# Token rows over 128 partitions, one row index per transfer, and first tokens turned by TensorE

## The chip, the cores and the metric

The kernel runs on one core of one Trainium2 chip. The time is the device time of one execution in microseconds; lower is better.

## What is computed

The inputs are `x` and a context `ctx`, both (32, 512, 512) in float32: 16384 tokens of 512 features. Reference, cut to what matters:

```python
def _L0_xattn_ref(q, k, v):               # k = v = ctx
    def step(r, kv_t):                    # along the 512 tokens of a batch row
        r = 0.9 * r + kv_t                # kv_t = k * v
        return (r, r)
    ...
    return q * jnp.swapaxes(rs, 0, 1)

def _L0_ffn_ref(x, ...):
    h = jnp.einsum('bsd,dh->bsh', x, W_exp) + b_exp        # 512 -> 2048
    h = butterfly(h, up_weights, D_HIDDEN)                 # 11 stages
    h = jax.nn.gelu(h + up_bias, approximate=False)
    h = butterfly(h, down_weights, D_HIDDEN)
    return jnp.einsum('bsh,hd->bsd', h, W_con) + b_con + down_bias

x = x + _L0_xattn_ref(_layernorm(x), ctx, ctx)
x = x + _L0_ffn_ref(_layernorm(x), ...)
```

## The kernel before

**Fold.** Both butterflies are linear, so the kernel first folds them into the two weight matrices: into W_exp (512 x 2048) and W_con (2048 x 512). This is the start, some 148 us. TensorE does it in steps listed in `FOLD` (line 310): step n writes bank n mod 3 of three PSUM banks, and ACT (for a few steps VectorE) copies the bank out; TensorE waits for the copy of step n-3. The kinds stand in this order: WT (transposes of W_exp), low_up, high_up, turn_high, high_dn, turn_low, back, low_dn, sixteen (or four) steps each. Between low_up and high_up the matrix goes through DRAM: SP stores 16 pieces (`up_low_folded`, line 539) and loads them as `Z` in four quarters (line 545). Between these copies ACT and VectorE round weights to a high and a low part (`weights_hi`, `weights_lo`), and SP stores them as `w1_products` in DRAM (line 569); W_con's parts go to `w2_split` (line 580).

**Tokens.** A tile is 512 tokens: G = 4 groups by J = 4 row indices by Q = 32 tokens by 512 features. Group g lies on partitions 32g to 32g+31; group g of tile t starts at token g*4096 + t*128. There are 32 tiles, so a tile takes 128 successive tokens from each of four far stretches. `token_rows` (line 73) gives the view (g, t, i, j, d). One transfer `rows[g, t]` moves 32 partitions by 4 row indices by 512: 256 KB; a tile takes four. Two tiles (h = 0, 1) form a super-block; there are U = 16, in two buffers `x0` and `x1`. Context tile h = 0 is loaded to `kv`, h = 1 to `raw`; ACT squares it (`square`, line 869), VectorE turns it in 32x32 blocks, scans with 0.9 and turns it back (`scan_chunk`, line 1200), multiplies by the normalised x (`gate`) and normalises again (`normalise`, line 1260): it writes to `kvT`, and a 32x32 transpose puts that to `kv`. Then the blocks must change partition group: `move_xT` (line 510) issues 4 transfers of 64 KB, and 16 moves bring one tile to `raw`, turned. For the first super-block SP issues half of them (lines 582 to 593) and GpSimd the other half (`first_moves`, line 777). `tokens_hi`, `tokens_lo` and `token_sum` make from `raw` the seven operands `xop` of a Strassen-like product; the third token operand that ACT rounds needs the first `token_sum`.

**The main loop.** Each super-block has NP = 8 steps p. A step has NM = 7 products (m = 0 to 6, six matmuls of 128x512 each, line 1739) and 8 down parts of six matmuls (lines 1760 and 1773), in a fixed order: product, part, product, part and so on, two parts last; product m starts as piece 2m of the step's 15. A product reads one of RING = 8 weight buffers `w1r`, a down part `w2r`, one of two buffers for a step. SP's program is one list in order; a DMA waits on the issue of those ahead of it:

```python
def refill(u, p, m, last):
    n = p * NM + m + RING
    ...
    sp.wait_ge(m_done, u * PER + (p * NM + m + 1))
    load_w1(n % PER, n % RING)
```

In step 0 SP first loads the next context tile h = 0 to `kv`, and after product 6 (in the first super-block elsewhere) the next tile h = 1 to `raw`; in step 1 after m = 2 it stores the 8 output transfers of the super-block before, after m = 5 it loads the 8 x transfers of the next; then follows the load of `w2r`. VectorE's `stats1` of the new x stands in step 2. In steps 4 and 6 SP issues 16 moves each. In the last super-block only the output is stored. At the end the rows of tile 0 are stored by GpSimd (line 845), and those of tile 1 by SP and ACT as they come, two transfers of 64 KB each per row index (`store_last_row`, line 501).

**ACT's queue.** All its DMAs are: five for the first coefficients, of 16x2, 16x16, 8x16, 4x16 and 2x16 separate runs (lines 478 to 484), one of 4 runs (line 488), two bias vectors of 16 runs each, two biases broadcast to 128 partitions, `hc_up` with 128x32 runs (line 928), and 8 last stores of 32 runs. A run is one contiguous piece on both sides.

Of the kernel before, what the change touches and what calls it, by code (L numbers as in the profile page):

```python
# [24 lines left out]
def xattn_ffn_program(nc, x_in, ctx_in, w_exp, b_exp, up_w, up_bias, down_w, w_con, b_con, down_bias, out):  # L25
# [16 lines left out]
    G = 4  # L42
# [13 lines left out]
    FIRST_MOVES = MOVES // 2  # L56
# [26 lines left out]
    with es:  # L83
# [195 lines left out]
        first_moved = [sem("first_xTa_moved"), sem("first_xTb_moved")]  # L279
# [15 lines left out]
        def moved_by(u):  # L295
            return u * (MOVES * NX) + FIRST_MOVES * NX
# [96 lines left out]
        def kept(kind, i, bank):  # L393
# [12 lines left out]
            if kind == "turn_low":  # L406
                return LX[:, 1, 4 * i:4 * i + 4, :].rearrange("p a b -> p (a b)"), whole
            assert kind == "back"
# [107 lines left out]
        def _(sp):  # L516
            def load_tokens(dst, h, rows, t, loaded):
                for g in range(G):
                    sp.dma_start(dst[Q * g:Q * g + Q, J * h:J * h + J, :], rows[g, t]).then_inc(loaded, NX)
# [71 lines left out]
            sp.wait_ge(xn_turned, 2 * J)  # L591
            move_xT(sp, 1, 0, xT_moved[1])
            move_xT(sp, 1, 1, xT_moved[1])
# [14 lines left out]
            def store(u, par):  # L608
                for h in range(2):
# [4 lines left out]
                    for g in range(G):  # L614
                        sp.dma_start(out_rows[g, u * 2 + h], xs[par][Q * g:Q * g + Q, J * h:J * h + J, :])\
                          .then_inc(out_stored, NX)

            def load_x(u, par):
                wait(sp, out_stored, (u - 1) * (2 * G * NX))
# [3 lines left out]
            def body(u, par, first, last):  # L623
                go = not last
                for p in range(NP):
# [3 lines left out]
                    for m in range(NM):  # L629
# [7 lines left out]
                        if first and p == 0 and m == 4:  # L637
                            sp.wait_ge(first_moved[1], FIRST_MOVES * NX)
                            sp.wait_ge(xT_moved[1], moved_by(u))
# [19 lines left out]
                        if go and p == 4 and m < G:  # L659
                            if m == 0:  # L660
                                sp.wait_ge(xlo_ready, (u + 1) * NM)
                                sp.wait_ge(xn_turned, (u + 1) * (2 * J) + J)
                            move_xT(sp, 0, m, xT_moved[0])
                    if go and p == NP - 2:
                        sp.wait_ge(xn_turned, (u + 1) * (2 * J) + 2 * J)
# [8 lines left out]
            for j in range(J):  # L674
                store_last_row(sp, j, (0, 1))
# [1189 lines left out]
```

## Time and profile before

| | us |
|---|---|
| runs (3): median, lowest, highest | 2779.0, 2778.31, 2779.04 |
| the profiled execution, its own time | 2779.58 |
| its span, first to last instruction | 2777.8 |
| TensorE busy (matmuls) | 2739.9, 99% |
| VectorE busy | 2129.9, 77% |
| ACT busy | 1127.5, 41% |
| GpSimd busy | 401.5, 14% |
| SP queue's transfers, share of 16 DMA engines | 64.8% |

The busy shares are averages over a start of about 148 us in which the weights are folded, a main loop, and an end. The mean granted clock of TensorE is 0.993 of full speed.

### The profile page before, as it was taken

The numbers are of one execution on the slowest core, as the hardware profiler recorded it, in microseconds if no ns is written. First come the engines' busy times: TensorE is split into PE (matmuls) and PEld (weight loads), VectorE is DVE, ScalarE is ACT, GpSimd is POOL, SyncE is SP. The second block draws the span as 40 slices with busy tenths as digits, with TensorE's granted clock in tenths as the row PEclk, the third lists the DMA queues.
The fourth block names the chain that finished last, engine by engine and source line by source line (L and its number), as shares of the span: only waits on it lengthen the run. The fifth ranks groups of instructions, "written<-read, shape, count | busy, mean of one in ns | idle before, by whom it ended". The sixth has DMA issues, their size and how long they took to land.

```text
span 2777.8 us, 35037 instructions
## 1 busy us (share of the span) xinstructions
PE 2739.9 (99%) x12159; PEld 2259.3 (81%) x12159; DVE 2129.9 (77%) x3562; ACT 1127.5 (41%) x1707; POOL 401.5 (14%) x577
## 2 busy tenths in 40 slices
PE   8889999999999999999999999999999999999999
PEld 6668888888888888888888888888888888888887
DVE  8968787787878778787877878777787877788533
ACT  5653434334343443434343343433434343343432
POOL 4821011110101101010110201011020111101000
PEclk8999999999999999999999999999999999999999
DMA  9795675758567575856758475675847657585543
GB/s 272 261 294 176 195 201 174 217 154 252 158 199 205 167 225 154 236 171 191 212 164 233 153 223 183 179 221 160 241 151 222 186 173 225 159 243 152 183 151 99
DMA packets 294837, 542.57 MB, mean 195 GB/s; under 512 B 37430, under 2 KB 101078, under 8 KB 277766
## 3 DMA queue, kind: packets, MB, share of 16 engines
q1 hardware_dynamic: 287760, 536.82, 64.8%
q0 software_dynamic: 1488, 2.27, 0.4%
q10 hardware_dynamic: 5414, 1.25, 0.3%
q8 instruction: 99, 1.62, 0.3%
q14 instruction: 76, 0.62, 0.1%
HBM read 445.83 MB, written 60.82 MB: 182 GB/s over the span
## 4 chain that ended last, share of the span: by engine, by line
PE 94%; DVE 1%; POOL 0%; DMA 0%; ACT 0%; issue 0%; ACTq 0%; DVEq 0%; POOLq 0%
PE ps L1739 44%; PE ps L1760 25%; PE ps L1773 25%; DMA raw<-kv 0%; PE ps L1634 0%; PE ps L1840 0%; DVE w1r L1195 0%; DVE xop L1195 0%; DVE x L1252 0%; POOL raw L512 0%; DVE raw L1249 0%; DVE st L1255 0%; POOL x L760 0%; ACT xop L904 0%; PE ps L1639 0%
## 5 line engine op out<-in xcount | busy, mean ns | idle before, releaser
L1739 PE MATMUL ps<-xop,w1r 128*128 128x512 f32 x5376 | 1364.1, 389 | 2.5 <-DVE xop L1283 1.6
L1739 PEld LDWEIGHTS ps<-xop,w1r 128*128 128x128 f32 x5376 | 1008.9, 188 | 213.0 <-DVE xop L1283 2.3
L1760 PE MATMUL ps<-w2r,ghi 128*128 128x512 f32 x2048 | 630.5, 389 | 0.0
L1773 PE MATMUL ps<-w2r,ghi 128*128 128x512 f32 x2032 | 625.8, 389 | 0.0
L995 ACT ACTIVATE st<-ps 128x512 f32<-128x512 f32 x384 | 229.7, 598 | 839.8 <-PE ps L1739 839.8
L1389 DVE TENSOR_TENSOR x<-ps,x 128x512 f32<-128x512 f32 x508 | 348.9, 687 | 280.9 <-PE ps L1773 278.5
L1760 PEld LDWEIGHTS ps<-w2r,ghi 128*128 128x128 f32 x2048 | 384.4, 188 | 79.8
L1773 PEld LDWEIGHTS ps<-w2r,ghi 128*128 128x128 f32 x2032 | 381.2, 188 | 79.8 <-DVE glo L1412 0.4
L1407 DVE TENSOR_TENSOR g<-ps,st 128x512 f32<-128x512 f32 x384 | 262.8, 684 | 212.1 <-PE ps L1739 212.1
L999 ACT ACTIVATE g<-g,gelu_bias 128x512 f32<-128x512 f32 x384 | 275.4, 717 | 362.6 <-DVE g L1407 361.7
L1412 DVE TENSOR_TENSOR glo<-g,ghi 128x512 fp32r<-128x512 f32 x510 | 347.6, 702 | 79.2 <-ACT ghi L1013 79.2
L1760 PE MATMUL ps<-w2r,glo 128*128 128x512 f32 x1024 | 398.3, 389 | 0.0
L1773 PE MATMUL ps<-w2r,glo 128*128 128x512 f32 x1016 | 395.2, 389 | 0.0
L1013 ACT ACTIVATE ghi<-g 128x512 fp32r<-128x512 f32 x512 | 310.0, 629 | 12.2
L1006 ACT ACTIVATE g<-ps,gelu_bias 128x512 f32<-128x512 f32 x128 | 88.3, 690 | 355.5 <-PE ps L1739 355.5
L1760 PEld LDWEIGHTS ps<-w2r,glo 128*128 128x128 f32 x1024 | 192.2, 188 | 39.9
L1773 PEld LDWEIGHTS ps<-w2r,glo 128*128 128x128 f32 x1016 | 190.7, 188 | 39.6
L760 POOL TENSOR_TENSOR x<-x,bias_row 128x512 f32<-128x512 f32 x128 | 167.9, 1313 | 251.5 <-DVE kvT L1274 230.1
L743 POOL TENSOR_TENSOR ve<-mv,eps 128x4 f32<-128x4 f32 x32 | 11.4, 356 | 1250.1 <-DVE mv L1230 1250.1
L1216 DVE TENSOR_TENSOR_SCAN kvT<-decay,kvT 128x512 f32<-128x512 f32 x128 | 157.2, 1228 | 4.4
L1283 DVE TENSOR_TENSOR xop<-raw,xop 128x1024 fp32r<-128x1024 f32 x112 | 136.2, 1227 | 2.6 <-ACT xop L904 2.6
L904 ACT ACTIVATE xop<-raw 128x1024 fp32r<-128x1024 f32 x112 | 116.1, 1051 | 7.2 <-DVE raw L1299 7.2
(171 smaller groups left out, 1620.0 us busy)
## 6 DMA issues: line engine op xcount, KB each, us to landing
w1r<-w_products SPq DMA_DIRECT2D x889, 256.0 KB, 3.3
w2r<-w_split SPq DMA_DIRECT2D x126, 1024.0 KB, 4.9
x<-in_x_dram SPq DMA_DIRECT2D x128, 256.0 KB, 7.3
raw<-kv SPq DMA_DIRECT2D x496, 64.0 KB, 2.1
out_dram<-x SPq DMA_DIRECT2D x120, 256.0 KB, 4.1
kv<-in_ctx_dram SPq DMA_DIRECT2D x64, 256.0 KB, 7.4
raw<-in_ctx_dram SPq DMA_DIRECT2D x64, 256.0 KB, 5.4
wexp<-in_L_ffn_W_exp_dram SPq DMA_DIRECT2D x4, 1024.0 KB, 11.0
```

What stands on the lines that cost most here:

```text
L760: nc.gpsimd.tensor_tensor(out=x[:, J * h + j, :], in0=x[:, J * h + j, :], in1=bias_row[:, :], op=ALU.add).then_inc(bias_added, 1)
L995: act.activation(st[:, i, :], bank[:, :], ACT.Copy).then_inc(copied, 1)
L999: act.activation(g32[:, q, :], g32[:, q, :], ACT.Gelu, bias=gelu_bias[:, k:k + 1])\
L1013: act.activation(ghi[:, p % 2, q, :], g32[:, q, :], ACT.Copy).then_inc(ghi_ready, 1)
L1216: nc.vector.tensor_tensor_scan(out=flat, data0=decay[:, :], data1=flat, initial=0.0, op0=ALU.mult, op1=ALU.add).then_inc(scanned, 1)
L1283: nc.vector.tensor_tensor(out=xop[:, XPOS[m], 1, :, :], in0=x_source(m), in1=xop[:, XPOS[m], 0, :, :].bitcast(f32), op=ALU.subtract).then_ ...
L1389: nc.vector.tensor_tensor(out=x[:, J + j, :], in0=ps_yb[:, :], in1=x[:, J + j, :], op=ALU.add)\
L1407: nc.vector.tensor_tensor(out=by_chunk(g32[:, q, :]), in0=by_token(bank[:, :]), in1=by_token(st[:, i, :]), op=ALU.add).then_inc(h_ready, 1)
L1412: nc.vector.tensor_tensor(out=glo[:, p % 2, q, :], in0=g32[:, q, :], in1=ghi[:, p % 2, q, :].bitcast(f32), op=ALU.subtract).then_inc(glo_r ...
L1739: last = nc.tensor.matmul(bank[:, :], w1r[:, slot, w, c * P:(c + 1) * P], xop[:, XPOS[m], v, c, :], start=(opens and i == 0), stop=(i == l ...
L1760: last = nc.tensor.matmul(ps_ya[j][:, :], g[:, p % 2, q, j * P:(j + 1) * P], w2r[:, p % 2, kk, w, :], start=(p == 0 and kk == 0 and i == 0 ...
L1773: last = nc.tensor.matmul(ps_yb[:, :], g[:, p % 2, q, j * P:(j + 1) * P], w2r[:, p % 2, kk, w, :], start=(kk == 0 and i == 0), stop=(kk == ...
```

## The change

Three parts. (1) Every token transfer (ctx, x, output) takes one row index j of all 128 partitions, again 256 KB and again four per tile. The last stores take 64 partitions in one transfer in place of two of 32. (2) For the first super-block the moves are gone from SP and GpSimd: `normalise` writes plain rows to `kv`, TensorE transposes them in eight new fold steps `tokens` (four 128x128 blocks each), and ACT copies each step's bank to `raw`. Waits on the moves become waits on these copies. (3) Counts of semaphores follow.

```diff
         def store_last_row(eng, j, groups):
...
-            for g in groups:
-                eng.dma_start(out_rows[g, end * 2 + 1][:, j, :], xs[end % 2][Q * g:Q * g + Q, J + j, :])\
-                  .then_inc(out_stored, NX)
+            eng.dma_start(out_rows[groups, end * 2 + 1, :, j, :],
+                          xs[end % 2][Q * groups.start:Q * groups.stop, J + j, :]).then_inc(out_stored, NX)
...
             def load_tokens(dst, h, rows, t, loaded):
-                for g in range(G):
-                    sp.dma_start(dst[Q * g:Q * g + Q, J * h:J * h + J, :], rows[g, t]).then_inc(loaded, NX)
+                for j in range(J):
+                    sp.dma_start(dst[:, J * h + j, :], rows[:, t, :, j, :]).then_inc(loaded, NX)
...
-                    for g in range(G):
-                        sp.dma_start(out_rows[g, u * 2 + h], xs[par][Q * g:Q * g + Q, J * h:J * h + J, :])\
-                          .then_inc(out_stored, NX)
+                    for j in range(J):
+                        sp.dma_start(out_rows[:, u * 2 + h, :, j, :], xs[par][:, J * h + j, :]).then_inc(out_stored, NX)
...
-            for g in range(G):
-                pool.dma_start(out_rows[g, end * 2], xs[end % 2][Q * g:Q * g + Q, 0:J, :]).then_inc(last_stored, NX)
+            for j in range(J):
+                pool.dma_start(out_rows[:, end * 2, :, j, :], xs[end % 2][:, j, :]).then_inc(last_stored, NX)
```

```diff
-        FOLD += [("high_dn", r, "act") for r in range(R)]
+        FOLD += [("high_dn", r, "act") for r in range(R - 3)]
+        FOLD += [("tokens", i, "act") for i in range(2)]
+        FOLD += [("high_dn", r, "act") for r in range(R - 3, R)]
+        FOLD += [("tokens", i, "act") for i in range(2, J)]
         FOLD += [("turn_low", q, "act") for q in range(KH // 4)]
-        FOLD += [("back", k, "act") for k in range(KH)]
+        FOLD += [("back", k, "act") for k in range(10)]
+        FOLD += [("tokens", i, "act") for i in range(J, J + 2)]
+        FOLD += [("back", k, "act") for k in range(10, KH)]
+        FOLD += [("tokens", i, "act") for i in range(J + 2, 2 * J)]
...
-            sp.wait_ge(xn_turned, J)
-            move_xT(sp, 0, 0, xT_moved[0])
-            move_xT(sp, 0, 1, xT_moved[0])
...
-            first_moves(0)
...
+                    elif kind == "tokens":
+                        last = nc.tensor.transpose(o, kv[:, i % J, block_c], ident[:, :])
```

**SP, from the context load of super-block 1 to its w2r load.** `kv`, `raw` and `x` are token buffers, `w1r` and `w2r` weight buffers; the size is that of the destination. Before:

```order
L519 DMA kv<-in_ctx_dram 32x4x512 x4
L555 DMA w1r<-w_products 128x512 x7
L519 DMA raw<-in_ctx_dram 32x4x512 x4
L562 DMA w2r<-w_split 128x2048
L555 DMA w1r<-w_products 128x512 x3
L615 DMA out_dram<-x 32x4x512 x8
L555 DMA w1r<-w_products 128x512 x3
L519 DMA x<-in_x_dram 32x4x512 x8
L555 DMA w1r<-w_products 128x512
L562 DMA w2r<-w_split 128x2048
```

With the change:

```order
L528 DMA kv<-in_ctx_dram 128x1x512 x4
L564 DMA w1r<-w_products 128x512 x7
L528 DMA raw<-in_ctx_dram 128x1x512 x4
L571 DMA w2r<-w_split 128x2048
L564 DMA w1r<-w_products 128x512 x3
L618 DMA out_dram<-x 4x32x512 x8
L564 DMA w1r<-w_products 128x512 x3
L528 DMA x<-in_x_dram 128x1x512 x8
L564 DMA w1r<-w_products 128x512
L571 DMA w2r<-w_split 128x2048
```

The order and the count of transfers stay; a load's destination now begins with 128 partitions, and an output transfer's, in DRAM, with 4 groups (and its source with 128 partitions; the DRAM side of a load likewise with 4 groups).

**SP in the start, from the last coefficient load to the first stores of rounded weights.** Before:

```order
L488 DMA WT<-in_L_ffn_down_weights_dram 4x1024
L545 DMA Z<-up_low_folded 128x2048 x4
L519 DMA raw<-in_ctx_dram 32x4x512 x4
L552 DMA wcon<-in_L_ffn_W_con_dram 128x4096 x2
L512 DMA raw<-kv 32x4x128 x8
L569 DMA w_products<-xop 128x2x512
```

With the change:

```order
L498 DMA WT<-in_L_ffn_down_weights_dram 4x1024
L554 DMA Z<-up_low_folded 128x2048 x4
L528 DMA raw<-in_ctx_dram 128x1x512 x4
L561 DMA wcon<-in_L_ffn_W_con_dram 128x4096 x2
L578 DMA w_products<-xop 128x2x512
L578 DMA w_products<-xop 128x512
```

The eight moves of the first tile are gone from their place behind `wcon`; the next eight, further on, too.

**ACT in the start, from the last high_dn copies (written to `Z`) to the first back copies (written to `wcon`).** Before:

```order
L867 ACTIVATE Z<-ps 128x64x8 x4
L889 ACTIVATE xop<-W1f 128x2x256
L889 ACTIVATE xop<-W1f 128x256
L889 ACTIVATE xop<-stmp 128x4x256
L867 ACTIVATE LX<-ps 128x512 x4
L867 ACTIVATE wcon<-ps 128x512 x4
```

With the change:

```order
L861 ACTIVATE Z<-ps 128x64x8
L861 ACTIVATE raw<-ps 128x16x32 x2
L861 ACTIVATE Z<-ps 128x64x8 x3
L861 ACTIVATE raw<-ps 128x16x32 x2
L883 ACTIVATE xop<-W1f 128x2x256
L883 ACTIVATE xop<-W1f 128x256
L883 ACTIVATE xop<-stmp 128x4x256
L861 ACTIVATE LX<-ps 128x512 x4
L861 ACTIVATE wcon<-ps 128x512 x4
```

Four token copies (to `raw`) stand ahead of a group of rounded weights (`xop<-W1f`, `xop<-stmp`); four more stand behind the tenth and the sixteenth back copy.

## Rows read from the trace of the kernel before

**Rows 1.** Page, part 1: engine, busy us, share of the span, instructions
```profile
PE 2739.9 (99%) x12159; PEld 2259.3 (81%) x12159; DVE 2129.9 (77%) x3562; ACT 1127.5 (41%) x1707; POOL 401.5 (14%) x577
```

**Rows 2.** Busy time by stretch, then TensorE's granted clock, DMA share, GB/s
```profile
196.20:359.40 163.20, 163.20 (x720) 134.53 (x719) 130.53 (x222) 64.82 (x97) 19.66 (x28) 1.00 0.67 196
351.00:359.40 8.40, 8.40 (x39) 6.96 (x38) 5.42 (x10) 2.31 (x4) 0.00 (x0) 1.00 1.02 244
364.00:370.00 6.00, 6.00 (x28) 4.96 (x27) 5.22 (x10) 1.36 (x2) 0.73 (x2) 1.00 1.00 381
200.00:2760.00 2560.00, 2560.00 (x11294) 2119.17 (x11293) 1955.57 (x3296) 1007.63 (x1514) 296.66 (x420) 1.00 0.64 190
```

**Rows 3.** TensorE, timeline: start us, us busy, line, operation [idle before]
```profile
144.16 0.76 PE L1639 MATMUL ps<-w2s,neg_ident 128*128 128x512 f32 x1 [7.75 <-ACT w2s L860]
...
168.57 1.61 PE L1739 MATMUL ps<-xop,w1r 128*128 128x512 f32 x6 [0.87 <-ACT g L1006]
...
311.98 1.52 PE L1739 MATMUL ps<-xop,w1r 128*128 128x512 f32 x6
313.34 0.61 PE L1760 MATMUL ps<-w2r,ghi 128*128 128x512 f32 x2
```

**Rows 4.** SP queue's DMA issues in super-block 1, timeline
```profile
312.54 2.02 SPq L519 DMA_DIRECT2D kv<-in_ctx_dram  x4
...
330.22 1.86 SPq L519 DMA_DIRECT2D raw<-in_ctx_dram  x4
...
339.74 8.13 SPq L615 DMA_DIRECT2D out_dram<-x  x8
...
350.94 3.65 SPq L519 DMA_DIRECT2D x<-in_x_dram  x8
```

**Rows 5.** VectorE, timeline in super-block 1
```profile
359.29 2.47 DVE L1237 BATCH_NORM_STATS2 st<-x 128x6 f32<-128x512 f32 x4 [0.17 <-DMA x<-in_x_dram]
```

**Rows 6.** Page, part 3: DMA queue, packets, MB, share of 16 engines (q10 is ACT's)
```profile
q10 hardware_dynamic: 5414, 1.25, 0.3%
```

**Rows 7.** Page, part 6: DMA issues, count, KB each, median us to landing
```profile
w1r<-w_products SPq DMA_DIRECT2D x889, 256.0 KB, 3.3
w2r<-w_split SPq DMA_DIRECT2D x126, 1024.0 KB, 4.9
```

**Rows 8.** Stretches of 1 us: TensorE busy, granted clock, DMA share, GB/s
```profile
141.00:142.00 1.00, 0.00 (x0) 0.50 1.06 404
147.00:148.00 1.00, 1.00 (x3) 0.61 1.03 414
```

**Rows 9.** SP queue's DMA issues in the start and the first super-block
```profile
31.47 13.92 SPq L539 DMA_DIRECT2D up_low_folded<-low_folded  x16
...
47.70 2.07 SPq L545 DMA_DIRECT2D Z<-up_low_folded  x4
...
158.98 3.17 SPq L519 DMA_DIRECT2D kv<-in_ctx_dram  x4
...
184.29 3.68 SPq L519 DMA_DIRECT2D x<-in_x_dram  x8
```

**Rows 10.** ACT, timeline in the start
```profile
68.33 1.90 ACT L871 ACTIVATE raw<-raw 128x2048 f32<-128x2048 f32 x1
...
108.81 1.06 ACT L889 ACTIVATE xop<-stmp 128x1024 fp32r<-128x1024 f32 x1 [2.38 <-DMA w_products<-xop]
...
122.76 3.02 ACT L867 ACTIVATE wcon<-ps 128x512 f32<-128x512 f32 x6
...
142.47 1.06 ACT L904 ACTIVATE xop<-raw 128x1024 fp32r<-128x1024 f32 x1 [7.24 <-DVE raw L1299]
```

**Rows 11.** Chain that ended last, in order of time: start us, us, what
```profile
134.17 7.02 DMA raw<-kv
```

**Rows 12.** SP queue, timeline at the end
```profile
2767.70 7.65 SPq L505 DMA_DIRECT2D out_dram<-x  x8
```

**Rows 13.** DMA issues of 351 to 355 us: count, KB, median us to landing
```profile
w1r<-w_products SPq DMA_DIRECT2D x1, 256.0 KB, 10.0
```

More of the change, by code:

```diff
@@ L407, in kept @@
                 return LX[:, 1, 4 * i:4 * i + 4, :].rearrange("p a b -> p (a b)"), whole
+            if kind == "tokens":
+                return raw[:, i // J, :, :].rearrange("p c (g j i) -> p c g j i", g=G, j=J)[:, :, :, i % J, :],\
+                    whole.rearrange("p (c g i) -> p c g i", c=KD, g=G)
             assert kind == "back"
@@ L893, in tokens_hi @@
                     act.wait_ge(m_done, u * PER + (m + 1 - NM))
-                if first and m == 0:
-                    act.wait_ge(first_moved[0], FIRST_MOVES * NX)
                 if m in (0, 1):
-                    act.wait_ge(xT_moved[0], moved_by(u))
+                    if first:
+                        wait_kept(act, "tokens", J - 1)
+                    else:
+                        act.wait_ge(xT_moved[0], moved_by(u))
                 elif m == 5:
                     if first:
-                        act.wait_ge(first_moved[1], FIRST_MOVES * NX)
-                    act.wait_ge(xT_moved[1], moved_by(u))
+                        wait_kept(act, "tokens", 2 * J - 1)
+                    else:
+                        act.wait_ge(xT_moved[1], moved_by(u))
                 else:
@@ L960, in _ @@
             weights_hi(3)
-            for r in range(12, R):
+            fold_step("high_dn", 12)
+            for i in range(2):
+                fold_step("tokens", i)
+            for r in range(13, R):
                 fold_step("high_dn", r)
+            for i in range(2, J):
+                fold_step("tokens", i)
             weights_hi(4)
@@ L970, in _ @@
                 fold_step("back", k)
+            for i in range(J, J + 2):
+                fold_step("tokens", i)
             weights_hi(6)
@@ L973, in _ @@
                 fold_step("back", k)
+            for i in range(J + 2, 2 * J):
+                fold_step("tokens", i)
             tokens_hi(0, 0, True)
@@ L1080, in _ @@
             for j in range(J):
-                store_last_row(act, j, (2, 3))
+                store_last_row(act, j, slice(G // 2, G))
         @block.vector
@@ L1290, in token_sum @@
                     if first:
-                        dve.wait_ge(first_moved[1], FIRST_MOVES * NX)
-                    dve.wait_ge(xT_moved[1], moved_by(u))
+                        wait_kept(dve, "tokens", 2 * J - 1)
+                    else:
+                        dve.wait_ge(xT_moved[1], moved_by(u))
                     dve.wait_ge(xlo_ready, u * NM + 1)
@@ L1641, in fold_step @@
                     return
+                if kind == "tokens":
+                    pe.wait_ge(xn_ready, i + 1)
                 for c in range(4):
@@ L1704, in _ @@
                 fold_step("high_dn", r)
+                if r == R - 4:
+                    for i in range(2):
+                        fold_step("tokens", i)
+            for i in range(2, J):
+                fold_step("tokens", i)
             pe.wait_ge(low_matrix_ready, 2)
@@ L1711, in _ @@
             for k in range(KH):
+                if k == 10:
+                    for i in range(J, J + 2):
+                        fold_step("tokens", i)
                 fold_step("back", k)
+            for i in range(J + 2, 2 * J):
+                fold_step("tokens", i)
             wait_kept(pe, "turn_low", KH // 4 - 1)
```

65 lines of the change are left out of this document (31 added, 34 removed).

## The prediction

> **What bounds the kernel now.** I read the page's busy times first, then the windows of one super-block (two token tiles, 1024 tokens), the SP queue's timeline, the DMA parts, and last the start and the tail. TensorE is busy 99% of the span [rows 1]; in a window of one super-block it is busy all of 163.20 us with its clock at 1.00 [rows 2]. That is 120 pieces (56 products, 64 down parts) of 1.36 us each [rows 3]. Nothing else ends late: a change shows in steady state only if it makes TensorE wait. Outside that, the start holds idle time, and about 6 us of tail follow the last addition.
>
> The SP queue feeds TensorE. Product n+8 of weights is loaded when product n is done, so a load has eight products, some 23 us, to arrive. Behind each other in the same queue stand, per super-block, 24 token transfers of 256 KB: ctx 4 + 4, output 8, x 8 [rows 4]. The first product of super-block 1 starts at 311.98 [rows 3]; a step p takes 15 pieces, 20.4 us. So product (p=2, m=4) is due at 311.98+40.8+10.9 = 363.7 and (3,0) at 373.2. The x load is already just in time: VectorE waited 0.17 us for it at 359.29 [rows 5].
>
> **How many DMA engines a transfer uses.** The page's packets tell it. The ACT queue shows 5414 packets [rows 6]. From the shapes its data make 5156: 32+256+128+64+32+4 for the coefficients, 32 for two bias vectors, 256 for two broadcasts, 4096 for hc_up, 256 for the last stores. The other 258 are completions. Counting 16 for each of the 15 transfers whose outermost dimension is 16, 32 or 128, and 8, 4, 2 and 4 for the four with so many rows, gives 240+18 = 258 exactly; 16 for all would be 304. So a transfer runs on as many of the 16 engines as its outermost dimension allows. A token transfer has now 32 rows outermost on both sides. After the change DRAM's side is 4 groups x 32 rows x 512, SBUF's 128 partitions: SBUF alone would allow 16 engines, DRAM 4. No row shows such a mixed pair, so 4 and 16 are the two ends; I take 4, because a share must be the same piece on both sides, and the same four each time, as the dearer of two unknowns (fours that took turns would be rival 1's case). The last stores fall to 2 x 32 x 512, two engines.
>
> The Trainium skill, page "DMA: Bandwidth & Descriptors", section "Why a DMA increments its semaphore by 16 and not by 1", says the engine count is the largest up to 16 that divides both sides' slowest dimension, and that hardware queues use the lowest-numbered ones. By that rule the count is 4, always the same four; the trace agrees where both sides are equal. The Trainium skill's same page, section "Rules for kernel authors", recommends 128 partitions for most bandwidth; by that alone the time would be that of the first rival.
>
> **The price of a token transfer.** From 364 to 370 the engines are fully busy at 381 GB/s [rows 2]: 23.8 GB/s each. On four engines 262,144 bytes are 65,536 each, 2.75 us. A weight load (256 KB on 16) takes 0.69 us of each engine, w2r (1 MB) 2.75. Bounds: w2r's median landing is 1.6 us after w1r's (4.9 against 3.3 [rows 7]) for 48 KB more per engine, so 64 KB take at least about 2.1 us; over the whole steady state engines move 190 GB/s at a share of 0.64 [rows 2], 18.6 each, so about 3.5. I take 2.75, the row of plain 2 KB rows. An engine's queue is in order, so the weight loads' shares on those four wait behind tokens. After its own 0.69 a load needs 3.3-0.69 = 2.6 us to land.
>
> **A middle super-block, at super-block 1's times.** The ctx load into raw is issued at 330.22 [rows 4]. The four engines then have: raw 4x2.75 to 341.2; w2r to 344.0; three weight loads to 346.0; 8 stores, 22.0, to 368.0; three weight loads to 370.1; 8 x loads, 22.0, to 392.1; the weights of product (3,0) to 392.8, landed at 395.4. The first weight load behind the stores lands at 368.7+2.6 = 371.3, 7.6 late for (2,4); that lateness is part of the larger one: (3,0) is 395.4-373.2 = 22.2 late. The w2r behind it lands at 398.2, TensorE asks at 396.8: 1.4 more. The first half of x lands at about 383.7 in place of 359; VectorE stands in its statistics until then, but releases TensorE for (3,0) no later than about 395, so that wait lies beside the first. The clock: in the start TensorE stood idle for 7.75 us until 144.16 [rows 3]; the granted clock reads 0.50 (1.2 of 2.4 GHz) in the slice from 141 and still 0.61 in that from 147 [rows 8]. So some 3.5 us ran at half speed, 1.75 lost; the same after a 22 us stop. Sum 25.3 us, times 14 middle super-blocks = 355. The last one has stores only: 49.9+2.6 after its start against 51.7 due, 1.
>
> **The first super-block.** From 159 until the x loads of 184.29 [rows 9] SP issues ctx (11), ctx (11), eight w2 stores of 512 KB at 1.38 (11) and nine weight loads (6.2): the four engines are busy until 198, with x until 220, and the weights of (3,0) land at 223.5. Step 1 starts at 168.57 [rows 3], so they are due 40.8 later, at 209.4: 14 late, with w2r and clock 17.
>
> **The start.** w_exp's 4 MB (11 us at 381 GB/s) occupy the engines to about 14, then kv 11, x 22 and about 1 of small loads: 48, where SP begins the stores of low_up at 31.47 now [rows 9]. The 16 stores land at 48+11+2.6 = 61.6, and Z's loads, issued at 47.70 now, start 14 late. Z 11 and ctx 11 then end at 83.6, landed 86.2; ACT squares that tile in order at 68.33 [rows 10] and holds the fold behind it: 18 late. Z's first quarter lands near 67, some 9 after its use begins now; that lies inside. Part of ACT's wait may be won back later: +17.
>
> **What the fold change gives.** It removes the first 16+16 moves from SP and POOL (the last of them is issued at 134.17 and lands 7.02 later [rows 11]) and 8 VectorE transposes; it adds 32 TensorE transposes (8 groups of about 0.5 us, in gaps where TensorE waits for ACT) and 8 ACT copies of 0.5 (six take 3.02 [rows 10]). Four copies fall into ACT's 2.38 us wait at 108.81 [rows 10]. The other four push ACT's arrival at the third token operand from 135.2 to 137.2. It started at 142.47, after 7.24 idle [rows 10]. What is late next is VectorE: ACT's last weight rounding ends 2 later, near 135, then come 1.2 for that group, a fold and 1.2 for the token difference: 137.9. Gain 4.6, plus 0.9 for a clock that need not fall: 5.5. If that cover is gone the copies cost 2 us.
>
> **The tail.** Last stores: 8 transfers of 128 KB on two engines, 65,536 bytes each, 2.75: from 2767.70 [rows 12] to 2789.7, landed 2792, before about 2777.8: +14.
>
> **Sum.** The profiled execution took 2779.58, its span 2777.8, the median of the runs 2779.0. 2779.6+355+1+17+17+14-5.5 = **3178 us**.
>
> **Rivals.**
> 1. All 16 engines serve the new shape. Then 2779.6-5.5-1 (the last for half as many last stores to issue): **2773 us**, faster. For it: SBUF's side is 128 rows, and today's 32-partition loads run at only 244 GB/s while the engines are fully busy [rows 2], so wide ones could be better. It decides if the engine count follows SBUF. Against it: the count of completions. 0.10.
> 2. Four engines, but weight loads overtake token transfers. Then only x is late: stores 22 and half of x 11 from 339.74 end at 372.7, landed 375.3; VectorE gets TensorE going about 4.5 later, 379.8, where it would have stopped at 367.8: 12 per super-block, 168; with 10 for the first, start, tail and gain **2983 us**. Against it: the weight load behind the x loads now took 10.0 us to land [rows 13], the median 3.3. 0.06.
> 3. Each engine is also slower on one block of partitions, as the 32-partition loads are now: 244 GB/s at 1.02 [rows 2], 15 GB/s, 4.4 us each. 24x1.63 = 39 more, 64 per super-block: about **3740 us**. 0.05.
>
> **How the numbers follow.** The forecast, 0.79. With 2.1 us per transfer and no clock loss a super-block loses about 7, in all about 2905; with 3.5 us it loses 43, in all a little over 3400. The range 2900 to 3400 holds most of the forecast, and rival 2: 0.8. A measurement tells 0.2% (5.6 us) from no change. Faster 0.08 and same 0.02 come from rival 1, slower 0.90.
>
> **What would show it.** Queue packets in part 3: SP's completions fall from 16 to 4 per token transfer, 376 of them, so about 4,500 fewer besides the moves that went. Token transfers land after 10 us and more; TensorE waits for DMA w1r at m=4 of p=2 and at p=3 in every super-block, and the granted clock drops after each; windows of one super-block last about 188 us. In the start, the square of ctx tile 1 near 86. Wrong if TensorE stays at 163.2 per super-block (rival 1), or waits at p=2 for VectorE alone (rival 2).

## The result, and the profile after

The changed kernel takes 3270.0 us (median of 4 runs, 3265.5 to 3271.8), the kernel before in the same session 2779.0. The ratio is 1.1768, with a 95% interval of 1.1753 to 1.1784. The profiled execution took 3269.3, its span 3267.4. The forecast was 3178 with a range of 2900 to 3400: slower, by the mechanism that was forecast, and 92 more than the sum. A fourth execution of the kernel before took 3442.9, where its other three took 2778.3 to 2779.0; it is left out as a slow one. Page, part 1, of the changed kernel:

```profile
PE 2852.6 (87%) x12191; PEld 2321.2 (71%) x12191; DVE 2119.3 (65%) x3554; ACT 1131.7 (35%) x1715; POOL 396.2 (12%) x561
```

TensorE's share falls from 99% to 87% [rows 1]. The following windows of the changed kernel give the stretch, TensorE's busy time, its granted clock, the DMA share and GB/s: 13 super-blocks, then a stretch in which almost only stores move, then one of the tail, in which only last stores do:

```profile
351.72:2870.07 2518.35, 2219.30 (x9362) 0.93 0.53 163
385.00:400.00 15.00, 15.00 (x68) 1.00 0.26 103
3249.00:3264.00 15.00, 0.00 (x0) 0.50 0.13 51
```

The second row is the price: a share of 0.26 is four engines of 16, and 103 GB/s are 25.8 each. The third reads 0.13, two engines, with 51 GB/s. In the kernel before the fully busy stretch gave 23.8 each [rows 2], which was the forecast's price.

Over the whole steady state I count from one load of `kv` to the next: 13 super-blocks between 351.72 and 2870.07, **193.7 us each, 30.5 more**. By the first row TensorE is busy 170.7 of them (2219.30 / 13), 7.5 more than the 163.20 of before, and idle 23.0, where it was never idle before. The 7.5 are the same matmuls at a lower clock. Against the fold change alone (first experiment, span 2770.6) the span is 496.8 longer: 26.0 until the first super-block's `kv` load (177.48 against 151.44), 20.8 in the first super-block, 14 x 30.5 = 427, and 22.7 in the last super-block and the tail.

Page, part 3 (queue: packets, MB, share of 16 engines), and the weight loads' row of part 6:

```profile
q1 hardware_dynamic: 280824, 535.75, 52.5%
...
q10 hardware_dynamic: 5294, 1.25, 0.2%
```

```profile
w1r<-w_products SPq DMA_DIRECT2D x889, 256.0 KB, 4.4
```

SP's queue falls from 287,760 packets to 280,824. The 6936 come out exactly: 376 token transfers with 4 completions in place of 16 (4512), four last stores with 2 in place of eight with 16 (120), and the 16 moves with 128 pieces and 16 completions each (2304). ACT's queue falls from 5414 [rows 6] by 120, its own last stores. Weights land after 4.4 in place of 3.3 [rows 7].

What TensorE waits for, by the view of waits (total, times, longest):

```profile
PE ps L1765 <- DMA w1r<-w_products: 175.4, 30, 9.7
PE ps L1799 <- DVE x L1401: 153.9, 15, 12.1
```

Super-block 1 of the changed kernel, which begins at 351: SP's timeline (start, duration, line, transfer), TensorE's and VectorE's. They answer to [rows 4], [rows 3] and [rows 5]. The last three rows are windows on the time behind TensorE's three stops, with the granted clock third from the end.

```profile
351.72 3.48 SPq L528 DMA_DIRECT2D kv<-in_ctx_dram  x4
...
369.40 3.56 SPq L528 DMA_DIRECT2D raw<-in_ctx_dram  x4
...
379.41 21.23 SPq L618 DMA_DIRECT2D out_dram<-x  x8
400.68 3.44 SPq L564 DMA_DIRECT2D w1r<-w_products  x3
411.59 11.10 SPq L528 DMA_DIRECT2D x<-in_x_dram  x8
```

```profile
412.23 2.93 PE L1765 MATMUL ps<-xop,w1r 128*128 128x512 f32 x6 [8.73 <-DMA w1r<-w_products]
...
429.25 1.22 PE L1799 MATMUL ps<-w2r,ghi 128*128 128x512 f32 x2 [9.75 <-DVE x L1401]
...
440.29 2.93 PE L1765 MATMUL ps<-xop,w1r 128*128 128x512 f32 x6 [3.95 <-DMA w1r<-w_products]
```

```profile
425.12 2.48 DVE L1242 BATCH_NORM_STATS2 st<-x 128x6 f32<-128x512 f32 x4 [26.33 <-DMA x<-in_x_dram]
```

```profile
412.20:418.20 6.00, 5.97 (x14) 0.50 0.23 74
429.20:432.20 3.00, 2.95 (x7) 0.52 1.01 261
440.20:446.20 6.00, 5.92 (x15) 0.54 0.66 246
```

The eight stores take 21.23 to be issued, 2.65 each, close to the 2.54 that four engines need for one at 103 GB/s: SP itself is held at their pace. The weights behind them go out at 400.68, and TensorE stands 8.73 until 412.23, at step 2, m=4. x is issued at 411.59, once the stores have landed, 59.9 into the super-block where it was 38.4. VectorE has waited 26.33 for it at 425.12. Its next addition of a down part (L1401) starts behind these statistics, at 428.51, and TensorE waits 9.75 for that. Then TensorE waits 3.95 for the weights of step 3. Behind each of the three stops the clock reads 0.50 to 0.54 (1.2 of 2.4 GHz) for some 6, 3 and 6 us, so the six matmuls behind the first and the third take 2.93 in place of 1.52 [rows 3], and the two behind the second 1.22 in place of 0.61. These 15 us at half speed lose some 7 (an estimate from the three windows).

### The profile page after: what moved, and what is told of

Read it like the earlier page. It is cut to its first block and busy times, and to the rows that moved or that the text cites. A ratio compares the mean times of both kernels' runs of the same rounds, so it can differ in the third digit from the quotient of the medians.

```text
span 3267.4 us, 35064 instructions
## 1 busy us (share of the span) xinstructions
PE 2852.6 (87%) x12191; PEld 2321.2 (71%) x12191; DVE 2119.3 (65%) x3554; ACT 1131.7 (35%) x1715; POOL 396.2 (12%) x561
## 3 DMA queue, kind: packets, MB, share of 16 engines
q0 software_dynamic: 1744, 1.22, 0.2%
## 5 line engine op out<-in xcount | busy, mean ns | idle before, releaser
L1765 PE MATMUL ps<-xop,w1r 128*128 128x512 f32 x5376 | 1417.3, 400 | 184.4 <-DMA w1r<-w_products 175.4
L1765 PEld LDWEIGHTS ps<-xop,w1r 128*128 128x128 f32 x5376 | 1037.4, 194 | 422.0 <-DMA w1r<-w_products 188.4
L1799 PE MATMUL ps<-w2r,ghi 128*128 128x512 f32 x2032 | 642.2, 398 | 153.9 <-DVE x L1401 153.9
L1786 PE MATMUL ps<-w2r,ghi 128*128 128x512 f32 x2048 | 650.9, 400 | 4.1 <-DMA w2r<-w_split 4.1
L1799 PEld LDWEIGHTS ps<-w2r,ghi 128*128 128x128 f32 x2032 | 388.2, 192 | 241.3 <-DVE x L1401 160.7
L1401 DVE TENSOR_TENSOR x<-ps,x 128x512 f32<-128x512 f32 x508 | 347.7, 684 | 248.3 <-PE ps L1799 245.6
L1786 PEld LDWEIGHTS ps<-w2r,ghi 128*128 128x128 f32 x2048 | 397.4, 195 | 95.3 <-DMA w2r<-w_split 11.4
L1786 PE MATMUL ps<-w2r,glo 128*128 128x512 f32 x1024 | 406.1, 397 | 0.0
L1799 PE MATMUL ps<-w2r,glo 128*128 128x512 f32 x1016 | 402.5, 396 | 0.0
L1242 DVE BATCH_NORM_STATS2 st<-x 128x6 f32<-128x512 f32 x128 | 78.9, 679 | 378.9 <-DMA x<-in_x_dram 378.9
L1786 PEld LDWEIGHTS ps<-w2r,glo 128*128 128x128 f32 x1024 | 197.9, 193 | 42.7
L1799 PEld LDWEIGHTS ps<-w2r,glo 128*128 128x128 f32 x1016 | 195.1, 192 | 41.5
```

The source lines that it names most:

```text
L1401: nc.vector.tensor_tensor(out=x[:, J + j, :], in0=ps_yb[:, :], in1=x[:, J + j, :], op=ALU.add)\
L1765: last = nc.tensor.matmul(bank[:, :], w1r[:, slot, w, c * P:(c + 1) * P], xop[:, XPOS[m], v, c, :], start=(opens and i == 0), stop=(i == l ...
L1786: last = nc.tensor.matmul(ps_ya[j][:, :], g[:, p % 2, q, j * P:(j + 1) * P], w2r[:, p % 2, kk, w, :], start=(p == 0 and kk == 0 and i == 0 ...
L1799: last = nc.tensor.matmul(ps_yb[:, :], g[:, p % 2, q, j * P:(j + 1) * P], w2r[:, p % 2, kk, w, :], start=(kk == 0 and i == 0), stop=(kk == ...
```

## The experiments

All ratios are to the kernel before, with their 95% interval. "Steady" is the distance from one super-block to the next, "busy" what TensorE is busy of it; both are means over 13 super-blocks, from the `kv` load of super-block 1 to that of the last. The changed kernel has 193.7 and 170.7.

| | us | ratio | steady | busy |
|---|---|---|---|---|
| fold change only | 2773.0 | 0.9976 (0.9967 to 0.9986) | 163.2 | 163.2 |
| 128 rows outermost on both sides | 2771.1 | 0.9971 (0.9958 to 0.9983) | 163.2 | 163.2 |
| stores only | 2917.4 | 1.0496 (1.0475 to 1.0517) | 173.4 | 166.0 |
| loads only | 3027.8 | 1.0893 (1.0871 to 1.0914) | 178.1 | 167.9 |
| 64 partitions | 4194.7 | 1.5094 (1.5064 to 1.5125) | 252.6 | 174.9 |
| transfers spread | 3090.3 | 1.1122 (1.1103 to 1.1140) | 181.0 | 166.0 |
| transfers only, moves kept | 3277.7 | 1.1794 (1.1777 to 1.1812) | 193.7 | 170.4 |
| tail only | 2796.9 | 1.0064 (1.0049 to 1.0079) | | |
| ctx in groups of 32 | 3136.5 | 1.1292 (1.1250 to 1.1334) | 185.6 | 168.1 |
| x waits for its half | 3236.6 | 1.1652 (1.1618 to 1.1686) | 191.4 | 170.1 |
| stores by GpSimd | 3123.2 | 1.1244 (1.1211 to 1.1276) | 183.2 | 167.9 |
| tail, two engines only | 2791.3 | 1.0044 (1.0027 to 1.0061) | | |

**1. The fold change alone.** The changed kernel with the old transfers:

```diff
-                for j in range(J):
-                    sp.dma_start(dst[:, J * h + j, :], rows[:, t, :, j, :]).then_inc(loaded, NX)
+                for g in range(G):
+                    sp.dma_start(dst[Q * g:Q * g + Q, J * h:J * h + J, :], rows[g, t]).then_inc(loaded, NX)
```

and so for the stores and the last stores.

> The fold change alone: every token transfer and the last stores are as before (groups of 32 partitions), the first tokens are turned by TensorE. The prediction's term: 5.5 us less than before, about 2773.5, with the third rounded token operand of ACT near 138 where it stood at 142.5, and super-blocks of 163.2 us. Rival: the four ACT copies put in front of the last weights cost what the moves cost, 2779 plus or minus 3. Both: nothing of the 491 us remains, if the transfers are their cause.

It took 2773.0, 6.1 less than before (3.9 to 9.2 by the interval). ACT's timeline of this run, the first copies of turned tokens and the third token operand:

```profile
101.35 1.08 ACT L863 ACTIVATE raw<-ps 128x512 f32<-128x512 f32 x2
...
135.97 1.06 ACT L902 ACTIVATE xop<-raw 128x1024 fp32r<-128x1024 f32 x1 [0.71 <-DVE raw L1313]
```

The operand starts at 135.97, after 0.71 of waiting, where it started at 142.47 after 7.24 [rows 10]. What ends last there is now VectorE's token difference, as forecast. None of the 491 us is left: they come from the transfers.

**2. 128 rows outermost on both sides.** Still 128 partitions and one row index per transfer:

```diff
-        return a.rearrange("b s d -> (b s) d").rearrange("(g t j i) d -> g t i j d", g=G, t=T, j=J, i=Q)
+        return a.rearrange("b s d -> (b s) d").rearrange("(t p j) d -> t j p d", t=T, j=J)
...
-                    sp.dma_start(dst[:, J * h + j, :], rows[:, t, :, j, :]).then_inc(loaded, NX)
+                    sp.dma_start(dst[:, J * h + j, :], rows[t, j]).then_inc(loaded, NX)
```

> As the changed kernel, 128 partitions and one row index per transfer, but a tile is 512 successive tokens, so that DRAM's side is 128 rows outermost (stride four tokens) in place of 4 groups of 32. The scan then carries over other tokens than the reference's; the work is the same in kind and amount. Theory (the smaller of the two outermost dimensions sets the engine count): 16 completions per token transfer again, super-blocks of 163.2 us, about 2773 in all. Rival (128 partitions by one row, or their issue, are slow in themselves, whatever DRAM's side is): super-blocks of 194 us and about 3270.

It took 2771.1; its scan runs over other tokens, so it does not compute the reference. Its SP queue (part 3), a row of part 6 (median us to landing at the end), and a super-block as a window on TensorE:

```profile
q1 hardware_dynamic: 285392, 535.77, 60.6%
```

```profile
x<-in_x_dram SPq DMA_DIRECT2D x128, 256.0 KB, 5.7
```

```profile
305.64:468.84 163.20, 163.20 (x722) 1.00 0.61 194
```

SP's queue has 4568 packets more than the changed kernel's: 376 x 12 for 16 completions again, and 4 x 14 for the last stores, now 64 rows. TensorE is busy all of 163.20. The width on the chip's side is harmless; DRAM's 4 groups outermost make the whole loss. The run also makes a tile one stretch of DRAM in place of four far ones; that it is the count of engines and not the distance is shown by the completions here and by the changed kernel's share of 0.26. With all engines these transfers even land a little sooner than the old ones: x after 5.7 in place of 7.3, `kv` after 5.9 in place of 7.4.

**3 and 4. Stores alone, loads alone.** In each, the fold change stays and the other kind is as in experiment 1.

> Fold change, and the 8 output stores per super-block over 128 partitions; loads and last stores as before. Four-engine theory: the stores take about 21 us, the weights behind them are some 8.7 us late as in the changed kernel; the x loads wait for the stores to have landed, then come over 16 engines, so that VectorE has its first half about 7 us earlier than in the changed kernel and TensorE waits some 3 for it; nothing at step 3. With the clock 17 per super-block, 14 of them, about 3010 (2960 to 3060). Rival (all 24 transfers cost alike, a third of 491 us): about 2940.

> Fold change, and the 16 token loads per super-block over 128 partitions; stores as before. Four-engine theory: x is issued where it was, its first half lands some 5 late, of which TensorE sees about 1, the weights of step 3 stand 1 to 2 late: 3 per super-block, 45 in all, with 17 for the start and 17 for the first super-block about 2850 (2810 to 2900). So stores alone and loads alone give together less than the changed kernel, because there x waits for slow stores. Rival (all transfers cost alike, two thirds of 491): about 3100.

Both missed: 2917 where I expected about 3010, and 3028 where I expected 2850. Stores only, SP and TensorE in super-block 1, which begins at 303.23:

```profile
330.43 13.62 SPq L619 DMA_DIRECT2D out_dram<-x  x8
...
355.01 3.66 SPq L529 DMA_DIRECT2D x<-in_x_dram  x8
```

```profile
355.66 1.66 PE L1766 MATMUL ps<-xop,w1r 128*128 128x512 f32 x6 [1.14 <-DMA w1r<-w_products]
...
365.99 1.22 PE L1800 MATMUL ps<-w2r,ghi 128*128 128x512 f32 x2 [5.96 <-DVE x L1402]
```

Loads only, the same for its super-block from 350.99:

```profile
378.35 9.02 SPq L619 DMA_DIRECT2D out_dram<-x  x8
...
395.40 10.65 SPq L529 DMA_DIRECT2D x<-in_x_dram  x8
```

```profile
412.75 1.22 PE L1801 MATMUL ps<-w2r,ghi 128*128 128x512 f32 x2 [6.24 <-DVE x L1403]
...
424.35 2.60 PE L1767 MATMUL ps<-xop,w1r 128*128 128x512 f32 x6 [3.45 <-DMA w1r<-w_products]
```

With stores alone the weights at step 2 are 1.14 late, not 8.7. In the changed kernel the ctx load into `raw`, four slow transfers, stands ahead of the stores; the expectation left its part in the 8.7 out. TensorE stops 5.96 for VectorE, where some 3 were expected. A super-block lasts 10.2 more than before, where 17 were expected. With loads alone that backlog delays the fast stores, and they delay x: it goes out 44.4 into the super-block, not 38.4, and TensorE waits 6.24 and 3.45. Above experiment 1's 2773 the two cost 144 and 255, together 399 of the 497: the rest is the tail (24, experiment 8) and what one backlog does to the other.

**5. Two engines.** Each token transfer in two, of 64 partitions and 128 KB:

```diff
-                    sp.dma_start(dst[:, J * h + j, :], rows[:, t, :, j, :]).then_inc(loaded, NX)
+                    for a in (0, 2):
+                        sp.dma_start(dst[Q * a:Q * a + 2 * Q, J * h + j, :], rows[a:a + 2, t, :, j, :]).then_inc(loaded, NX)
```

> As the changed kernel, but each token transfer is cut into two of 64 partitions (2 groups by 32 rows in DRAM, 128 KB each); the last stores stay. Theory (the smaller outermost dimension sets the engines, here 2): each half takes as long as a whole one does now, 2.65 us, and there are twice as many, so all backlogs double: the weights behind the stores some 47 late, then waits of 20 and 11, with the clock about 86 lost per super-block, 250 us each, about 4140 in all (3900 to 4400). Rival (the width in partitions is what costs, and narrower is better): between the kernel before and the changed one, about 3020. Rival (a transfer costs a fixed time to issue): twice the transfers by 2.65, but the weight loads not late; under 3700.

It took 4194.7, 252.6 per super-block (a stretch of stores, then one super-block, as windows on TensorE; then its waits):

```profile
1255.00:1275.00 20.00, 5.76 (x26) 0.70 0.13 51
1189.30:1441.80 252.50, 175.73 (x721) 0.83 0.40 125
```

```profile
PE ps L1768 <- DMA w1r<-w_products: 641.6, 30, 30.9
PE ps L1802 <- DVE x L1404: 306.1, 15, 21.3
PE ps L1768 <- ACT g L1014: 195.4, 29, 10.2
```

The share is 0.13: two engines at 25.5 GB/s. By the total over 15 super-blocks each waits 42.8 for weights, where 47 and 11 were expected, 20.4 for VectorE as expected, and 13.0 for ACT, which was not expected and which I did not follow. The sum is 76 for 78; the clock costs 11.7 (busy 174.9), where 8 were left for it. Narrower was not better, and both rivals fall.

**6. The transfers spread.** Each tile's stores count on a semaphore of their own:

```diff
                         if p == 1 and m == 2 and not first:
-                            store(u - 1, 1 - par)
+                            store(u - 1, 1 - par, (0,))
+                        if p == 2 and m == 2 and not first:
+                            store(u - 1, 1 - par, (1,))
+                        if go and p == 3 and m == 0 and not first:
+                            load_x(u + 1, 1 - par, (1,))
```

> The changed kernel with its slow transfers apart, four at a time: stores of tile 0 at step 1, x loads of tile 0 behind them once those have landed (a semaphore of their own), stores of tile 1 at step 2, x loads of tile 1 at step 3. Theory (what costs is the backlog in front of the weights and the wait of x for all eight stores, not the total of four-engine work, some 124 of 163 us): the waits at steps 2 (weights) and 3 go, x of tile 0 lands some 14 late in place of 26 and stops TensorE once for about 8, with one loss of clock: 9.5 per super-block, about 2970 (2930 to 3010). Rival (the four engines' throughput bounds the super-block): 3200 or more.

It took 3090.3. SP and TensorE in the super-block from 1074.25:

```profile
1124.66 2.45 SPq L529 DMA_DIRECT2D x<-in_x_dram  x4
```

```profile
1145.59 1.22 PE L1805 MATMUL ps<-w2r,ghi 128*128 128x512 f32 x2 [15.01 <-DVE x L1407]
```

The waits for weights in the steady state are gone: 7.4 us in one place are left of 175.4. So the throughput of four engines is not the bound. One stop remains, 15.01 and not 8: x goes out 50.4 into the super-block, and VectorE has it at 1141.46, 20.5 later in the super-block than in the kernel before, where 14 were expected. That is 16.8 after the issue, where four transfers of 2.65 make 10.6. What took the rest wasn't tried. A super-block lasts 17.8 more than before and not 9.5: about 15 idle and 2.8 of clock. The change in this form still costs 311.

**7. The transfers alone.** The kernel before with the new transfers and last stores, its moves kept.

> The kernel before with all token transfers and last stores over 128 partitions, its moves kept: the other half of the change. If the two halves add up, the changed kernel's 3270 plus the fold change's 6: 3276. Rival: with ctx and Z late in the start the moves are hidden, and the fold change gives nothing there: 3270. Super-blocks of about 193.7 us in both.

It took 3277.7, 7.7 more than the changed kernel. The two halves add up: -6.1 and +498.7 make 492.6, against 491.0.

**8 and 12. The tail.** Experiment 8 is experiment 1 with all the new last stores; in 12 GpSimd's four are back in groups of 32.

> Fold change, and only the last stores (SP's and ACT's over 64 partitions, GpSimd's over 128); all others in groups of 32. Prediction's term for the tail, 8 stores of 128 KB on two engines: 14 more than with the old last stores, 2787. Rival (they are the same four engines' work only in queue length, and the stores come 3 us apart anyway as rows become ready): 2 to 4 more, 2776.

> Fold change, and of the tail only SP's and ACT's last stores over 64 partitions; GpSimd's four stores of tile 0 are back in groups of 32 partitions. With both over the wide shape the tail cost 24 more than the fold change alone, where the prediction had 14. If the missing 10 are GpSimd's wide stores, which run beside the others on the same two engines: 8 x 65,536 bytes at 25.5 GB/s are 20.6, the end 15 later than with the fold change alone, about 2788. If two engines are slower than that by themselves: 2797.

They took 2796.9 and 2791.3: 23.9 and 18.3 above the fold change alone. Windows on TensorE, the DMA share and GB/s at the end, of 8 and then of 12:

```profile
2776.00:2794.00 18.00, 0.00 (x0) 0.50 0.13 50
```

```profile
2766.00:2769.00 3.00, 0.00 (x0) 1.00 0.57 164
2772.00:2788.00 16.00, 0.00 (x0) 0.50 0.13 51
```

At the end two engines work by themselves at 50 and 51 GB/s. 8 x 65,536 bytes at 25.5 take 20.6, and the end of 12 is 19.7 after experiment 1's (2790.3 against 2770.6), where I expected 15: in the first us GpSimd's stores move beside them. GpSimd's wide ones add 5.5 more. The 2797 is above both of my values for experiment 8, and 2791 lies between those for 12. How the engines divide the first us wasn't tried.

**9. ctx alone in groups of 32.** The loader takes the old form where the rows are those of ctx.

> The changed kernel with its ctx loads alone back in groups of 32 partitions; x and all stores stay over 128. Theory (one order per engine: the ctx load into raw stands ahead of the stores and makes the weights behind them late): the wait for weights at step 2 falls from 8.7 to about 1, as with stores alone; x is issued some 52 into the super-block in place of 60, so TensorE waits about 12.6 for VectorE and 4 for the weights of step 3; with the clock some 22.7 per super-block, start 5, first super-block 6, tail 25: about 3125 (3090 to 3160). Rival (costs of kinds of transfers add up: 144 for stores, half of 255 for x, 24 for the tail): 3070.

It took 3136.5. TensorE in super-block 1, from 326.74:

```profile
379.01 1.67 PE L1769 MATMUL ps<-xop,w1r 128*128 128x512 f32 x6 [0.98 <-DMA w1r<-w_products]
...
395.74 1.22 PE L1803 MATMUL ps<-w2r,ghi 128*128 128x512 f32 x2 [12.31 <-DVE x L1405]
...
407.74 2.93 PE L1769 MATMUL ps<-xop,w1r 128*128 128x512 f32 x6 [4.44 <-DMA w1r<-w_products]
```

0.98, 12.31 and 4.44, where I expected 1, 12.6 and 4, and 22.4 more per super-block, where I expected 22.7. This shows what experiment 3 missed: the ctx backlog is what makes the weights behind the stores late. The rival, costs that add up by kind, falls.

**10. x waits for its half only.**

```diff
-                wait(sp, out_stored, (u - 1) * (2 * J * NX))
                 for h in range(2):
+                    wait(sp, out_stored if h else out_stored_a, (u - 1) * (J * NX))
```

> The changed kernel, but the x loads of tile 0 wait for the four stores of tile 0 alone (a semaphore of their own), those of tile 1 for the other four; order and places stay. Theory (the backlog is the cause, the wait for landed stores adds only a round trip): x lands 1.5 to 2.5 sooner, 25 to 35 in all, about 3240. Rival (the wait itself, 7.5 between the weight loads and x's issue, is a cost): 100 less, about 3170.

It took 3236.6, 33.4 less than the changed kernel, 2.4 per super-block. That x's first half waits for the other half's stores too is a small part; the backlog is the cause.

**11. The stores by GpSimd.** The eight stores move from SP's program to GpSimd's, at the same point:

```diff
-                            store(u - 1, 1 - par)
...
+                    for j in range(J):
+                        pool.dma_start(out_rows[:, (u - 1) * 2 + h, :, j, :], xs[(u - 1) % 2][:, J * h + j, :])\
+                            .then_inc(out_stored, NX)
```

> The changed kernel with the 8 output stores of each super-block issued by GpSimd and not by SP, at the same point of the program; the last rows' stores have a semaphore of their own. If an engine takes what comes in one order, whatever the queue: waits as in the changed kernel (8.7, 10.5 and 3.4 per super-block), about 3270. If an engine serves queues in turn: no wait for weights at step 2; x is issued no sooner, so TensorE waits about 21 for VectorE in one piece; one loss of clock less, about 3240. The waits tell it, not the time. A slower VectorE beside GpSimd's transfers would add to both.

It took 3123.2. The DMA share and GB/s while these stores run, as windows on TensorE, and TensorE's stops in the super-block from 354.38:

```profile
385.00:388.00 3.00, 3.00 (x15) 1.00 1.05 363
388.00:391.00 3.00, 3.00 (x15) 1.00 1.04 297
```

```profile
419.86 1.22 PE L1809 MATMUL ps<-w2r,ghi 128*128 128x512 f32 x2 [10.12 <-DVE x L1411]
...
430.85 2.93 PE L1775 MATMUL ps<-xop,w1r 128*128 128x512 f32 x6 [3.34 <-DMA w1r<-w_products]
```

GpSimd's queue between 384 and 402 (packets, MB, share of 16 engines):

```profile
q0 software_dynamic: 2176, 2.11, 42.5%
```

The wait for weights at step 2 is gone, as by the second hypothesis, but for another reason too: with SP's weight loads beside the stores the share is 1.04 and more and 297 to 363 GB/s move, where in the changed kernel the share is 0.26 from 385 to 400, while the same stores move. The eight stores' 2.11 MB alone take a share of 42.5% over 18 us, and four engines could give 25%. So GpSimd's stores of the same shape, eight in flight, are not held to the same four engines. The Trainium skill, page "DMA: Bandwidth & Descriptors", section "Why a DMA increments its semaphore by 16 and not by 1", says that GpSimd's queue gives such a transfer consecutive engines from a cursor that goes round, so that the next transfer gets others; the trace agrees with its share of 42.5%, and no run here shows the engines one by one, nor how many a single store had. So x goes out 47.6 into the super-block, not 59.9, and TensorE waits 10.12 and not 21. My 3240 was 117 too high, and whether queues take turns on an engine stays open: the run changed two things at once.

## Why the prediction was right, point by point

- **What bounds the kernel.** Right. Each super-block loses what TensorE waits and what its clock loses behind the waits; with the old transfers, or with 128 rows outermost, nothing is lost (experiments 1 and 2).
- **How many engines.** The forecast was 4, with 4 and 16 as the two ends. Shown three ways: the completions to the packet, the share of 0.26, and the return of all the time once DRAM has 128 rows outermost (experiment 2). With 2 groups it is two engines (experiment 5). That they are the same four for each transfer, the dearer of the two unknowns, fits the share: it stays at 0.26 while several stores stand in the queue. Rival 1 falls with that. The Trainium skill's page "DMA: Bandwidth & Descriptors" gives this rule in the section named in the prediction; the trace agrees, at 4 and at 2. The Trainium skill's advice of 128 partitions for bandwidth (same page, "Rules for kernel authors") is given together with at least 1 MiB per transfer; these have 256 KB. In experiment 2 the 128 partitions cost nothing, and with 4 groups outermost in DRAM they go with 18% more time.
- **The price.** Forecast 2.75 per transfer. 65,536 bytes at 25.8 GB/s are 2.54, and SP's issues stand 2.65 apart. Rival 3 (4.4) falls.
- **A middle super-block.** Forecast 25.3, measured 30.5. The waits were forecast at 22.2 + 1.4 = 23.6, and TensorE is idle 23.0. Of the totals in the view of waits some 7.2 for weights (6.4 in the first super-block, 0.9 in the last) and 5.7 for VectorE lie outside the 14 middle ones; these have 168.2 / 14 = 12.0 for weights and 148.2 / 14 = 10.6 for VectorE, **22.6**, and 0.4 in small waits. The weights at step 2 were forecast 7.6 late and wait 8.7; x was forecast at 383.7, 71.2 after the super-block's start, and came at 73.4.
- **The step that failed** is the term for the clock, 1.75 per super-block; it measured 7.5. It had two faults. The first is "so that wait lies beside the first": VectorE stops TensorE by itself between the two waits for weights, so there are three stops, where the sum priced one. The second is the price, taken from one place of the start as 3.5 us at half speed: the windows behind the three stops show some 6, 3 and 6. Experiments with fewer stops give the price per super-block: 2.8 with one stop of 6 us (stores alone, besides one of 1.1), 2.8 with one of 15 (experiment 6), 4.7 with two (loads alone, and experiment 11), 4.9 with two and one of 1.0 (experiment 9), 7.5 with three. So a stop of 3 us and more costs 2.3 to 2.8 here and not 1.75, and its length between 6 and 15 us hardly matters. Over 14 super-blocks the clock makes 81 more than forecast and the waits 8 less, and that is the missing 72.
- **What was luck in the waits.** The weights of (3,0) let TensorE go 88.6 after the super-block's ctx load (440.29 against 351.72), where 82.9 were forecast. TensorE, slowed by the clock, reached that product some 5.4 later than forecast too (88.6 less its 22.4 of waits are 66.1, where it was due at 60.7), so that the sum of its waits came out near 23.6. The sum did not count that x waits for the stores to have landed; experiment 10 gives 2.4 of it back. What else made the weights late was not followed.
- **Rival 2.** Its 2983, weights overtaking, falls: SP's weights waited. Its view of VectorE as a stop of its own was right, and belonged in the forecast.
- **The first super-block and the start.** Forecast 17 and 17, measured 20.8 and 26.0. In the first super-block TensorE waits 5.7 for VectorE and 6.4 for weights, again in two stops and not in one. SP in the start, first a row of the kernel before, then rows of the changed one:

```profile
3.28 4.75 SPq L519 DMA_DIRECT2D kv<-in_ctx_dram  x4
```

```profile
3.14 15.88 SPq L528 DMA_DIRECT2D kv<-in_ctx_dram  x4
19.06 8.52 SPq L508 DMA_DIRECT2D HX<-in_L_ffn_up_weights_dram  x15
...
64.15 2.08 SPq L554 DMA_DIRECT2D Z<-up_low_folded  x4
66.27 7.14 SPq L528 DMA_DIRECT2D raw<-in_ctx_dram  x4
...
177.48 2.95 SPq L528 DMA_DIRECT2D kv<-in_ctx_dram  x4
```

```profile
94.15 1.91 ACT L865 ACTIVATE raw<-raw 128x2048 f32<-128x2048 f32 x1 [14.01 <-DMA raw<-in_ctx_dram]
```

Z's loads go out at 64.15, where 61.6 was forecast, but the square of the ctx tile in `raw` starts at 94.15, not near 86, after 14.01 of waiting. SP was also held: its first four ctx loads took 15.88 to issue in place of 4.75, which moved the coefficient loads behind them from 8.07 to 19.06. The sum had counted only the engines. With ctx back in groups of 32 (experiment 9) the first `kv` load of the loop stands at 163.30: ctx causes 14.2 of the 26.0, and the other 11.8 are x's, since no output is stored there.
- **The fold change.** Forecast 5.5, measured 6.1.
- **The tail.** Forecast 14, measured 23.9 (experiment 8). The term did not count GpSimd's stores beside the others; the wide form of these makes 5.5 of it. Without it 18.3 are left (experiment 12), and where the last 4 come from stays open.
- **Sum.** From the fold change alone the forecast had 404 for the rest of the change, and 497 were measured: of the 93 between them 72 lie in the middle, 9 in the start, 4 in the first super-block, 8 in the last one and the tail.

Of the versions tried that compute the reference, the fold change with the old transfers is the fastest, 2773.0: 0.2% under the kernel before and 15% under the changed one.

## What to carry to other kernels

Look at the outermost dimension of both sides of a transfer, not at the number of partitions or bytes: 256 KB with 4 groups outermost in DRAM ran on four of 16 engines, and a queue in order made everything behind it late. Count the completions of a queue to see how many engines a shape gets. When a wait is to be priced, follow each later stop of the same stretch by itself: here every stop of 3 us and more cost 2.3 to 2.8 of clock besides its own length.

## What the hardware showed that I had not expected

- SP's issue itself is held when its engines have a backlog: 8 stores took 21.23 us to issue, in the kernel before 8.13 [rows 4]. With the ctx loads over 16 engines, so without that backlog ahead (experiment 3), they took 13.62.
- Eight stores of the same shape from GpSimd's queue spread over more than four engines: a share of 42.5% over 18 us in experiment 11, and with SP's loads beside them 297 to 363 GB/s, where a backlog of SP's stores gave 103.
- One engine gave 25.0 to 25.8 GB/s, whether two or four worked (50 and 51 GB/s in the tails, 103 in the main loop), while 16 gave 381 in all, 23.8 each [rows 2].
- With 16 engines, 128 partitions by one row index landed sooner than 32 by four: 5.7 (experiment 2) against 7.3 us (the kernel before) for x. Experiment 2 also reads other stretches of DRAM, so the shape alone is not shown as the cause.
